# A graph-attention kernel: transposed one-hot matrices from broadcast relative rows, compared in place on VectorE

## What is computed

```python
xn = layernorm(x)
xp = (xn @ W).reshape(n, 4, 64)
a_src, a_dst = einsum(xp, att_src), einsum(xp, att_dst)        # n x 4
e = leaky_relu(a_src[src] + a_dst[dst], 0.2)                   # edges and self loops
e_exp = exp(e - segment_max(e, dst)[dst])
alpha = e_exp / segment_sum(e_exp, dst)[dst]
gat = relu(segment_sum(alpha * xp[src], dst))
x = x + gat + mix(xn)                 # mix: linear attention over all nodes
x = x + experts(layernorm(x))         # 8 experts of 3 dense layers, softmax-weighted by one router
```

## Time and profile before

| | |
|---|---|
| median of 3 runs | 3340.61 us (3336.39 to 3344.05) |
| the profiled execution | 3340.92 us, its span 3339.1 us |
| mean granted TensorE clock | 0.867 |
| PE busy | 2875.5 us (86%), 18549 matmuls |
| VectorE (DVE) busy | 2209.1 us (66%) |
| ScalarE (ACT) busy | 1550.5 us (46%) |
| POOL busy | 1505.3 us (45%) |
| DMA | 316.34 MB, mean 95 GB/s |

### The profile page before, as it was taken

The page is one execution under the profiler, slowest core; times in us unless marked ns, Lnnn a source line. Parts: engine busy times, 40 slices in busy tenths (PEclk is TensorE's granted clock), DMA queues, the critical chain, the costliest instruction groups (busy, mean ns, idle before and its releaser), DMA issues. The chain is left out here.

```text
span 3339.1 us, 62774 instructions
## 1 busy us (share of the span) xinstructions
PE 2875.5 (86%) x18549; PEld 2173.3 (65%) x18549; DVE 2209.1 (66%) x6073; ACT 1550.5 (46%) x4109; POOL 1505.3 (45%) x1625
## 2 busy tenths in 40 slices
PE   5678887888887888888888888859999999999999
PEld 3567666667766776777777777745665656566655
DVE  5457787787887877887878888864444444545424
ACT  3245555555555565565565555533332333333332
POOL 0177777777777777777777777500000000000000
PEclk9777888887877888787788787869999999999999
DMA  7544444444444444444444444431001010101000
GB/s 245 171 138 121 126 121 121 123 124 123 124 115 114 125 129 125 128 122 124 128 127 127 126 124 123 101 128 34 22 24 45 1 45 0 45 1 45 1 12 11
DMA packets 163365, 316.34 MB, mean 95 GB/s; under 512 B 32208, under 2 KB 97360, under 8 KB 162896
## 3 DMA queue, kind: packets, MB, share of 16 engines
q0 software_dynamic: 75552, 212.96, 24.5%
q1 hardware_dynamic: 78576, 90.49, 8.5%
q10 hardware_dynamic: 8896, 8.82, 0.8%
HBM read 272.44 MB, written 39.70 MB: 93 GB/s over the span
## 5 line engine op out<-in xcount | busy, mean ns | idle before, releaser
L758 POOL DMA_INDIRECT xg<-edge_table,idx x1568 | 1490.3, 950 | 501.7 <-issue 485.3
L1024 PE MATMUL ps_y<-y,hotw 128*128 128x260 f32 x3520 | 909.3, 421 | 41.0 <-issue 37.9
L1024 PEld LDWEIGHTS ps_y<-y,hotw 128*128 128x128 f32 x3520 | 721.9, 212 | 201.1 <-issue 50.8
L1515 ACT ACTIVATE h<-ps_h,bnb,bns 128x448 f32<-128x448 f32 x448 | 324.1, 723 | 624.2 <-PE ps_h L1475 624.2
L1617 DVE SCALAR_TENSOR_TENSOR yb<-ps_ye,wts,yb 128x256 f32<-128x256 f32 x392 | 189.7, 484 | 576.0 <-PE ps_ye L1483 576.0
L891 ACT ACTIVATE y<-xg,w 128x65 f32 x1760 | 466.5, 338 | 7.4 <-ACT w L883 0.4
L1241 DVE TENSOR_TENSOR y<-xg,ps_v 128x780 f32<-128x780 f32 x440 | 418.1, 961 | 8.8
L940 ACT CAST hotw<-hot 128x512 f32<-128x512 bf16 x440 | 267.1, 622 | 272.8 <-PE ps_y L1024 271.8
L1475 PE MATMUL ps_h<-zt,w 128*128 128x448 f32 x896 | 362.3, 559 | 6.0 <-issue 5.7
L1483 PE MATMUL ps_ye<-wo,h 128*128 128x256 f32 x1568 | 348.1, 379 | 0.0
L1475 PE MATMUL ps_h<-h,w 128*128 128x448 f32 x896 | 345.9, 539 | 0.0
(11 more groups left out here) (231 smaller groups left out, 2880.5 us busy)
## 6 DMA issues: line engine op xcount, KB each, us to landing
xg<-edge_table,idx POOLq DMA_INDIRECT x1568
mix_rows<-kk SPq DMA_DIRECT2D x49, 257.0 KB
t<-mix_rows SPq DMA_DIRECT2D x7, 1799.0 KB, 7.6
xb<-xn_turned SPq DMA_DIRECT2D x50, 128.0 KB
x<-in_x SPq DMA_DIRECT2D x7, 896.0 KB, 8.0
xn_rows<-xn SPq DMA_DIRECT2D x7, 896.0 KB, 5.1
xn_turned<-xnt SPq DMA_DIRECT2D x7, 896.0 KB, 8.5
x7e<-in_x SPq DMA_DIRECT2D x7, 896.0 KB, 9.7
```

The lines of the kernel that those rows point to most:

```text
L758: pool.indirect_dma_start(xg[:, q * OCT + u, j, :], None, dr["table"], bass.IndirectOffsetOnAxis(ap=idx[q][:, c:c + 1], axis=0)).then_inc( ...
L1024: mm = pe.matmul(ps_y[v % 2][:, 0:RW], hotw[v % 2][:, j, :], y[v % 2][:, j, :], start=(j == 0), stop=(j == CH - 1))
L1515: act.activation((h1, h2)[layer][:, mh, half * HN:(half + 1) * HN], ps_h[g % 4][:, 0:HN], ACT.Relu, bias=K.bnb[:, layer, c:c + 1], scale=K ...
```

## The change

`hot_t` is no longer made by transposes and copies. prepare now also stores `rel` with one visit per row, 448 x 512 bf16, in HBM (`list_rel`): the first nodes of the blocks are turned into a column `bcol` by four more transposes, and VectorE subtracts them from `xrows`. In attend SP loads the 8 rows of the next step, 8 KB, into each of the 128 partitions of `hot_t` (1 MB written per step) once the lookup of the present step has read it. VectorE compares it in place with the number of the partition, in four parts of 128x1024, behind visits 4 to 7 of its loop; the four parts of step 0 come in the prologue. `turn`, `turned` and `ps_o` go, and the lookup waits for the four compares.

```diff
 prepare, SP
-                sp.wait_ge(stored, 16 * VT)
+                for t in range(VT):
+                    sp.wait_ge(relb_d, ONE + t + 1)
+                    sp.dma_start(dr["rel"][t * P:t * P + rows[t], :], relb[0:rows[t], t, :]).then_inc(stored, 16)
+                sp.wait_ge(stored, 16 * 2 * VT)
 prepare, PE, after block 5 of the first chunk
+                def turn_base():
+                    pe.wait_ge(gidx_d, ONE + 1)
+                    pe.wait_ge(base_d, ONE + 1)
+                    for t in range(VT):
+                        pe.transpose(ps_g[0:rows[t], t * P:(t + 1) * P], base[:, t * P:t * P + rows[t]], ident).then_inc(bt_d, 1)
 prepare, VectorE, columns() after block 0 of the second chunk; the subtract in casts(t)
+                def columns():
+                    dve.wait_ge(bt_d, ONE + VT)
+                    for t in range(VT):
+                        link(dve.tensor_copy(bcol[0:rows[t], t:t + 1], ps_g[0:rows[t], t * P:t * P + 1]))
+                    dve.engine_nop().then_inc(bcol_d, 1)
+                    dve.tensor_scalar(relb[0:r, t, :], xrows[0:r, t, 0:GE], bcol[0:r, t:t + 1], None, ALU.subtract).then_inc(relb_d, 1)
 attend, SP
+                def relative_in(s):
+                    sp.wait_ge(look_d, ONE + s)
+                    sp.dma_start(hot_t[:].rearrange("p v e -> p (v e)"),
+                                 dr["rel"][s * SV:(s + 1) * SV, :].rearrange("v e -> (v e)").partition_broadcast(P)).then_inc(hot_in, 16)
                     if p is not None and p + 1 < KP:
                         turned_in(p + 1)
-                        plain_in(p + 1)
                     if n(1) == FIN:
                         block_in(0)
+                    if n(1) < NS - 1:
+                        relative_in(n(1) + 1)
+                    if p is not None and p + 1 < KP:
+                        plain_in(p + 1)
                     for b in mixes(n(1)):
 attend, ScalarE
-                def turned(p, n):
-                    act.wait_ge(ho_d, ONE + n(SV // 2) + (p + 1))
-                    act.copy(hot_t[:, 2 * p:2 * p + 2, :].rearrange("p v n -> p (v n)"), ps_o[p % 2][:]).then_inc(ht_d, 1)
-                    for p in range(2):
-                        turned(p, n)
-                    for p in range(2, SV // 2):
-                        turned(p, n)
 attend, PE
-                    for p in range(2):
-                        turn(p, q, n)
-                    for p in range(2, SV // 2):
-                        turn(p, q, n)
-                    pe.wait_ge(ht_d, ONE + n(SV // 2) + SV // 2)
+                    pe.wait_ge(ht_d, ONE + n(4) + 4)
 attend, VectorE
+                        if v in (4, 5, 6, 7) and n(1) < NS - 1:
+                            equal(v - 4, n(1) + 1)
+                def equal(part, s):
+                    dve.wait_ge(hot_in, 16 * s + 16)
+                    at = hot_t[:, 2 * part:2 * part + 2, :]
+                    dve.tensor_scalar(at, at, K.cst[:, C_PART:C_PART + 1], None, ALU.is_equal).then_inc(ht_d, 1)
                 for p in range(PRE):
                     bias(p)
                     build(p, 0, 0)
+                    equal(p, 0)
```

More of the change, by code:

```diff
@@ L684, in attend @@
         xb_in, mix_out, xk_in, xn_in = m.sem("xb_in"), m.sem("mix_out"), m.sem("xk_in"), m.sem("xn_in")
-        ps_o = [m.ps(f"ps_o{i}", [P, 2 * CH * P], BF16) for i in range(2)]
         ps_y = [m.ps(f"ps_y{i}", [P, 512]) for i in range(2)]
@@ L809, in _ @@
                 plain_in(0)
+                relative_in(0)
                 sp.wait_ge(dbig_d, ONE + 1)
@@ L952, in _ @@
                 ident = K.cst[:, C_ID:C_ID + P]
-                def turn(p, q, n):
-                    pe.wait_ge(hot_d, ONE + n(4) + 4)
-                    pe.wait_ge(ht_d, ONE + n(SV // 2) + max(p - 1, 0))
-                    for v in (2 * p, 2 * p + 1):
-                        for j in range(CH):
-                            at = (v % 2 * CH + j) * P
-                            mm = pe.transpose(ps_o[p % 2][:, at:at + P], hot[q][:, v, j, :], K.cstb[:, 0:P])
-                    mm.then_inc(ho_d, 1)
                 def body(q, i, n):
```

22 lines of the change are left out of this document (15 added, 7 removed).

## The result

The kernel with the change takes 3406.8 us, the median of 4 runs (3403.2 to 3416.6); the kernel before takes 3341.4 us beside it (4 runs). The ratio is 1.0197, with a 95% interval of 1.0180 to 1.0213: **65 us slower**. The prediction said slower, 3366 us, in a range from 3342 to 3398 us. The sign was right and the size was 41 us short.

A forecast was written before the change was run, and what follows sets the result against it. The prediction took POOL's gather queue as the bound until step 37, then the step itself, with VectorE and TensorE nearly full; 12.6 - 1.5 + 8 + 4 + 1.5 = 24.6 us onto 3340.9 gave 3366 us, range 3342 to 3398.

The forecast's parts named there:

- Bounds, two regimes: Edge stage: POOL's gathers set the pace until step 37; from step 38 the step itself does, 35.2 us each.
- Removed: Transposes and copies before the lookup: almost nothing on the path, 0.09 us a step, 1.5 us over 17 steps.
- Added to VectorE: Four compares a step of 488 ns: 1.1 us per one-block step, 0.4 per two-block, 12.6 us in all; earlier nothing.
- (a) POOL beside the compares: Gathers up to step 37 stretched by VectorE's compares, 0.06 us each: 8 us, bounds zero and 72 us.
- The upper bound of 72 us: Gathers up to step 37: each compare stops POOL for its whole length; as a rival 3430 us, chance 0.07.
- (b) The load and the landings: The 1 MB load shares the gathers' DMA engines: 4 us more landing waits, between 0 and twice 10.8.
- SP's queue: block_in of two-block steps now stands behind the 1 MB load: some 6 us for both, in time, little to spare.
- the other case: Rival: block_in lands late, xb 1 to 4 us late in each two-block step, 3385 us, chance 0.12.
- The list stage: Added subtracts, copies, transposes and stores: about 3 us of VectorE work, half in gaps, 1.5 us ahead of POOL.
- the rival that the kernel gets faster: Late steps are TensorE's, not VectorE's, so removed transposes and lookup wait come back: 22 us less, 3320 us, chance 0.07.
- signs of being right: Lookup 0.1 us after pair, compares some 490 ns, late steps 35.9 us, ScalarE's POOL waits below 60, mean gather 955 ns or more.
- signs of being wrong: Late steps under 35.2 us, compares 760 ns or more, TensorE waiting for xb, last gather issued much later than 2160 us.

The follow-up runs named there:

- load_once: The changed kernel with the load of relative rows issued for step 0 alone, compares kept (output not the reference's): 3386.5 us, ratio 1.0128.
- in_waits_late: The changed kernel with two of four compares moved into VectorE's idle time and POOL's landing wait one gather later: 3372.6 us, ratio 1.0090.
- compares_alone: The kernel before with four in-place compares a step added on VectorE, transposes and copies kept, no load: 3376.9 us, ratio 1.0107.
- load_alone: The changed kernel with transposes and copies put back and compares taken out, the load of each step kept: 3388.6 us, ratio 1.0149.
- double_load: The changed kernel with each step's load of relative rows done twice, the second once the first has landed: 3506.1 us, ratio 1.0497.

## Why the prediction was wrong in size

**Bounds, two regimes.** Right. The split at step 37 holds in every kernel above, and POOL's queue sets the pace before it, in both kernels: its parts add up to the whole delay of the early part.

**Removed.** Right: 1.5 us. The lookup starts 0.1 us after pair in all steps, and the late steps' wait there fell by 0.09 us on the mean, the very figure that step 52 gave, which is luck for one step.

**Added to VectorE.** Right: 480 ns instead of 488 (the Trainium skill's VectorE: DVE Perf Modes, Mode 4×_2P, gave an estimate of about 480, and the trace agrees), 1.07 us in a one-block step and 0.4 to 0.5 in a two-block step, and 12.9 us in the late part (0.76 us x 17, steps 37 to 53, from the add of visit 3 to that of visit 7), where 12.6 stood. That before step 37 the same costs fall into ScalarE's waits for POOL, and cost nothing, came true too, within 2 us: with the compares and no load (load_once) the early part's 20.1 us are POOL's own but for 1.9, and two compares less on the visits brought nothing there (in_waits_late).

**(a) POOL beside the compares.** Right: 8 us up to step 37 stood there (its own factors give 8.6), and the gathers up to there are longer by 10.0 us after the change and by 9.2 in compares_alone. The upper bound of 72 us, at which the Trainium skill's rule (SBUF — State Buffer, Who interferes with whom) would have put it, was not reached: the 244 gathers that overlap a compare take 64 ns more than the others on the mean, and 157 of them stay within 1000 ns. Here the trace doesn't agree with a block of the whole length.

**(b) The load and the landings.** This is the step that failed. I took 4 us more, between 0 and twice the present 10.8 us. It measured 28.2 us of stalls up to step 37 after the change and 39.4 in load_alone, whose early part is 43.9 us later. The 5.2 us that POOL lost for room in the ring, in one place, are in no term either. The bound had no ground, for two reasons. First, I read the 10.8 us as waits; 33 of the 34 are the ordinary gap of 0.30 us, so the row said nothing of how a landing turns into lost time. Second, it was worked out from a trace without the load, when that trace had what was needed: the slack. POOL comes to the fourth gather 3.75 us after the end of the last gather of the group before (three gathers of 1.25 us), and starts it 0.78 us after a landing that it had to wait for. So a landing costs nothing if it comes within some 3.3 us of that end. In the kernel before a group lands after 1.9 us in the median. That leaves 1.4 us, and a group in flight beside the load of 1 MB, which takes 5.9 us, lands after 3.4 us in the median and after 6.3 at worst. It cost POOL 1.3 us on the mean, 37 times in 55 steps. The load's own transfer (5.9 us to landing) was forecast well, at 6; it was asked only whether the load itself would be in time, not what stands beside it.

**SP's queue.** Right: xb in time in all but one step, late there by 0.3 us. double_load, where one more load makes it 1.7 to 5.0 us late, shows how near the other case was.

**The list stage.** Right: 1.4 us (first gather 145.9 to 147.3 us) for 1.5. The kernels that share the new stage have 145.7 to 149.6 us there, so that it agrees to 0.1 us is luck.

**What was missing.** The wait ahead of ps_m. TensorE's clock was in the prediction only as a gain, in the rival that the kernel gets faster. The products between ps_f and ps_m run at 1.2 GHz in more steps than before, and ps_m starts 0.40 us later on the mean of steps 37 to 53, 6.8 us in 17 steps. With that the late part is 12.9 + 6.8 - 1.5 = 18.2 of 18.7 us measured.

**The signs.** Of the signs of being right the lookup, the compares and the mean gather (958 ns) came. Late steps take 36.3 us, not 35.9, and ScalarE's waits for POOL are 91.4 us, not below 60. One of the signs of being wrong came, and it points at (b): the last gather starts at 2216.7 us, far behind 2160.

## What to carry to other kernels

When a transfer is added beside a queue that binds, ask what slack that queue's own transfers have: the distance from issue to the wait for their landing, less the time they take, against the length of the new burst. If it is less, the wait is what to move, before the bytes: one gather of distance took 20.9 of the 28.2 us of stalls. Before a wait in a summary is used as a measure, look at the longest of its kind: 34 waits of 10.8 us were 33 ordinary gaps of 0.3 us. And a total of waits over a whole stage prices nothing; only those count that lie where their engine sets the pace. Work that a full engine is rid of may have kept its clock up for what comes next (1.16 to 2.08 us for eight products in step 30).

## What was not expected of the hardware

Beside a load of 1 MB, 8 KB a partition, a group of gathers lands 3.4 us after POOL's last instruction for it in the median, without one 1.9 us, in the same trace. Over all groups the median stays at 1.9 us and only the tail tells: one in ten took 3.6 us or more (2.7 before), at worst 6.3 us (5.2 before). And a chip of the same kind ran all five kernels sent to it 36 to 39% slower than they run on the others, with stalls of up to 19 us that no line of the profile explains.
